# Relu parts of a step put two steps ahead instead of one, in a kernel of 32 dependent steps on four engines

## What is computed

```python
idx = _knn_indices(xyz, K)                        # K = 8, xyz = ctx_4096 (4, 1601, 512)
for i in range(NUM_BLOCKS):                       # 4 blocks, run twice: 8 layers
    shortcut = points                             # (4, 256, 512)
    p = _lrelu(points)                            # slope 0.01
    g = _group_point(p, idx_t)
    c = jnp.einsum('oi,bin->bon', w_center[i], p)
    gn = jnp.einsum('oi,bikn->bokn', w_neighbor[i], g)    # same weights as w_center
    points = (c + gn.sum(axis=2)) / (K + 1.0) + shortcut
```

## Time and profile before

| | |
|---|---|
| time of the runs, median (range) | 353.4 us (353.21 to 355.57), 3 runs |
| the profiled execution's own time | 353.02 us |
| its span, first to last instruction | 351.2 us |
| TensorE busy | 336.7 us (96%) |
| VectorE busy | 239.8 us (68%) |
| ScalarE busy | 129.6 us (37%) |
| GpSimd busy | 84.8 us (24%) |
| granted TensorE clock | full in all 40 slices |

### The profile page before, as it was taken

The page is one execution under the profiler, slowest core; times in us unless marked ns, Lnnn a source line. Parts: engine busy times, 40 slices in busy tenths (PEclk is TensorE's granted clock), DMA queues, the critical chain, the costliest instruction groups (busy, mean ns, idle before and its releaser), DMA issues.

```text
span 351.2 us, 4578 instructions
## 1 busy us (share of the span) xinstructions
PE 336.7 (96%) x1816; PEld 268.3 (76%) x1816; DVE 239.8 (68%) x345; ACT 129.6 (37%) x197; POOL 84.8 (24%) x75
## 2 busy tenths in 40 slices
PE   5999999999999989988899899999999999999996
PEld 2667666666666778877788788888889888888984
DVE  0156378468457474999965877779598687779773
ACT  1116113120411224336445726463552626464410
POOL 2002000200200002225304605243251525235200
PEclk9999999999999999999999999999999999999999
DMA  7994433433120000000000000000000000000023
GB/s 254 336 329 188 149 120 121 149 119 121 55 94 0 3 0 3 0 0 2 0 2 0 0 2 0 3 1 0 2 0 3 0 2 0 2 0 0 10 112 119
DMA packets 7444, 20.20 MB, mean 58 GB/s; under 512 B 640, under 2 KB 1920, under 8 KB 6400
## 3 DMA queue, kind: packets, MB, share of 16 engines
q1 hardware_dynamic: 7424, 19.93, 16.7%
HBM read 17.83 MB, written 2.10 MB: 57 GB/s over the span
## 4 chain that ended last, share of the span: by engine, by line
PE 77%; DVE 13%; ACT 4%; issue 4%; DMA 1%; DVEq 1%
PE wide L249 30%; PE wide L334 24%; PE wide L323 7%; PE wide L312 6%; PE wide L314 6%; DVE y_rest L549 4%; DVE y_lo L553 3%; DVE r_mixed L473 3%; DVE state L561 2%; ACT y_hi L440 2%; PE wide L256 1%; ACT relu L432 1%; DMA points<-in_ctx_dram 1%; PE wide L300 1%; DVE gram L536 1%
## 5 line engine op out<-in xcount | busy, mean ns | idle before, releaser
L232 POOL TENSOR_TENSOR r_low<-relu,r_high 128x512 fp32r<-128x512 f32 x64 | 82.6, 1305 | 245.2 <-ACT r_high L435 245.2
L249 PE MATMUL wide<-points 128*128 128x512 f32 (+3 forms) x384 | 109.9, 440 | 4.1 <-DMA points<-in_ctx_dram 4.1
L334 PE MATMUL wide<-adj,y_hi 128*128 128x512 f32 (+1 forms) x260 | 101.6, 392 | 0.8 <-DVE state L561 0.8
L334 PE MATMUL wide<-adj,y_lo 128*128 128x512 f32 (+1 forms) x260 | 101.4, 391 | 0.0
L249 PEld LDWEIGHTS wide<-points 128*128 128x128 f32 x384 | 65.7, 192 | 38.5 <-issue 19.4
L549 DVE TENSOR_TENSOR y_rest<-wide,y_hi 128x1024 f32<-128x1024 f32 x32 | 39.1, 1221 | 43.5 <-ACT y_hi L440 43.5
L312 PE MATMUL wide<-w_high,r_high 128*128 128x256 f32 x256 | 62.9, 284 | 2.1 <-DVE y_rest L549 1.0
L314 PE MATMUL wide<-w_low,r_low 128*128 128x256 f32 x256 | 62.4, 281 | 0.0
L440 ACT CAST y_hi<-wide 128x1024 fp32r<-128x1024 f32 x32 | 32.2, 1008 | 68.5 <-PE wide L314 68.5
L334 PEld LDWEIGHTS wide<-adj,y_hi 128*128 128x128 f32 x260 | 48.9, 188 | 11.2 <-DVE state L561 1.2
L334 PEld LDWEIGHTS wide<-adj,y_lo 128*128 128x128 f32 x260 | 48.9, 188 | 9.9
(11 more groups left out here) (50 smaller groups left out, 141.9 us busy)
## 6 DMA issues: line engine op xcount, KB each, us to landing
points<-in_ctx_dram SPq DMA_DIRECT2D x8, 1024.0 KB, 5.2
points<-in_ctx_dram SPq DMA_DIRECT2D x8, 256.0 KB, 3.3
points<-in_ctx_dram SPq DMA_DIRECT2D x4, 512.0 KB, 5.5
state<-in_x_dram SPq DMA_DIRECT2D x4, 512.0 KB, 13.3
out_dram<-state SPq DMA_DIRECT2D x3, 512.0 KB, 2.8
rest<-in_ctx_dram SPq DMA_DIRECT2D x8, 128.0 KB, 5.2
w_raw<-in_fside_BxSxS_dram SPq DMA_DIRECT2D x1, 1024.0 KB, 12.6
last_row<-in_ctx_dram SPq DMA_DIRECT2D x1, 1024.0 KB, 16.9
```

Source lines behind the costliest of these rows:

```text
L232: nc.gpsimd.tensor_tensor(r_low[:, b, h, :], relu[:, h, :], r_high[:, b, h, :].bitcast(fp32), ALU.subtract).then_inc(r_low_ready, 1)
L249: mm = nc.tensor.matmul(bank[i][:, 0:N - i * P], points[:, t, i * P:(i + 1) * P], points[:, t, i * P:N], start=(t == 0), stop=False)
L334: mm = nc.tensor.matmul(bank[to][:, cols], part[:, s % 2, q, h * P:(h + 1) * P], adj[:, b, q, cols], start=(q == 0 and part is y_hi), stop ...
```

## The change

A new function `relus_at(s)` says which steps' relu parts stand in step s. Step n gets them two steps ahead (in step n - 2), unless its batch was last updated so late that they can only stand one step ahead: with the previous layer in step p, the place is step max(p + 2, n - 2). ScalarE's `relu_parts` and VectorE's `relu_mixed` both follow it. Their place inside a step is as before (ahead of `y_high(s)`; between the two updates), and TensorE's and GpSimd's instruction order is the same.

```diff
+        def relus_at(s):
+
+            return [n for n in range(B - 1, B * LAYERS)
+                    if s == max(n - 2 if STEPS[n][0] == 0 else step_before(n) + 2, n - 2)]
+
...
             for s in range(B * LAYERS):
-                if s + 1 >= B - 1 and s + 1 <= LAST_STEP:
-                    relu_parts(s + 1)
+                for n in relus_at(s):
+                    relu_parts(n)
                 y_high(s)
...
                     update(s - 1, 0, ALL, 2 * out_at(s - 1), 0)
-                if B - 1 <= s + 1 <= LAST_STEP:
-                    relu_mixed(s + 1)
+                for n in relus_at(s):
+                    relu_mixed(n)
                 if s > 0:
                     update(s - 1, 1, ALL, 2 * out_at(s - 1) + 1, 1)
```

## The result

| | before | with the change |
|---|---|---|
| median of the runs | 353.3 us (353.18 to 355.57, 4 runs) | 372.2 us (371.92 to 372.61, 4 runs) |
| span of the profiled execution | 351.2 us | 370.8 us |
| y_hi of step 0 starts (profiled) | 125.92 | 126.65 |
| from there to the end of the span | 225.3 us | 244.15 us |

The ratio is 1.052, with a 95% interval of 1.048 to 1.056: the change makes the kernel 5% slower. The forecast was 371 us, within 365 to 377. The part ahead of the loop isn't touched by the change, but its length differs from run to run with the first loads (y_hi of step 0 starts between 125.85 and 128.55 us in the profiles of this study), so I compare loops by the stretch from there to the end: 18.9 us more.

The account below looks back on a forecast made before the run. TensorE bounds before, the ring through all engines after. 2.5 us late at the start, 15.0 over six cycles and the end put main(30) 17.7 later: span 368.9, execution 370.7, median 371 us, range 365 to 377.

Parts of the forecast that it names:

- What bounds the kernel: Before the change, TensorE: 6.59 us a step alone, 19.77 for three, where the kernel takes 20.00.
- A to B: From y_hi of the step with two steps' relu parts (A) to the next step's (B): 8.31 us.
- the ring: Turn through all engines, y_hi, y_rest, y_lo, update, r_mixed, update, relu, back to y_hi: 7.17 us before the change.
- B to A': From y_hi of the one-part step (B), through the step with none (C), to the next two-part step (A'): 14.2 us.
- 2.5 us for every three steps: Steady cycle of three steps grows from 20.00 to 22.5 us; six whole cycles add 15.0 us.
- Start: Steps 5 to 9: a late y_hi(5) puts y_hi(9) at 195.3 instead of 192.79, 2.5 us late.
- End: y_hi(27) at 330.3, then 8.31 and 7.17 us to y_hi(29); main(30) at 348.2, 17.7 us later.
- The order of r_mixed and r_low: In the two-part step, VectorE's second r_mixed starts 0.35 us ahead of GpSimd's r_low; no time was added for it.
- the 380 us case: Rival, 7%: GpSimd's r_low gets the port before r_mixed, 1.3 us in each of seven cycles; about 380 us.
- The hold does not go round: Rival, 8%: y_hi of the two-part step is late, the next step's is not; 1.2 us in seven cycles, 362 us.
- Faster: Rival, 3%: r_mixed a step earlier gives back TensorE's 5.1 us of waits, or 3 to 4 of them; 350 us.
- The clock rival: Rival, 1%: TensorE's clock might fall from more waiting, giving far over 380 us.

Follow-up runs that it names:

- the run with two buffers: The change, with two relu buffers instead of one: 368.5 us, ratio 1.043 to the kernel before.
- only the steps four back: Against the kernel before, only steps whose batch was last updated four steps back get their parts a step earlier, on both engines: 354.5 us, ratio 1.003.
- the second r_mixed behind the update: The change, with the second r_mixed of a step behind the second update instead of ahead of it: 368.4 us, ratio 1.041 to the kernel before.
- steps five back alone: Against the kernel before, only steps whose batch was last updated five steps back get their parts a step earlier, on both engines: 370.1 us, ratio 1.048.
- ScalarE's part alone: ScalarE's relu parts as in the change, VectorE's r_mixed as in the kernel before: 370.6 us, ratio 1.049.
- VectorE's part alone: VectorE's r_mixed as in the change, ScalarE's relu parts as in the kernel before: 356.9 us, ratio 1.011.

## Why the prediction was right, point by point

- **What bounds the kernel.** Held. TensorE alone takes 6.59 us a step, and the three kernels that keep ScalarE's old order and only move r_mixed ran at 19.76 us for three.
- **A to B, 8.31 us.** Measured 8.28 in the change and 7.15 where one r_mixed was taken out of the link, as the ring's sum has it. What the link is worth is another matter: with nothing ahead of y_hi(B) A to C takes 12.25 us, with the change 12.87, so it adds 0.6 us. The prediction's times for main(C) say the same, 10.1 by TensorE and 10.7 by y_rest(B); measured were 10.15 and 10.68.
- **B to A', 14.2 us.** Measured 14.23 (4.59 + 9.64), but two of its terms were off and cancelled out, so the agreement within 0.03 us is partly luck. The relu of half 1 can't start at 9.81, because ScalarE is in half 0 until 10.25 (9.04 + 1.21): I left out the engine's own queue there. And I had GpSimd hold back the last relu only; the rows show it at the first relu of the second step too, and smaller in all: 0.29 us of wait in the row at 262.15, and 0.47 us a cycle by the run with two buffers, where the prediction had 13.0 - 12.2 = 0.8.
- **2.5 us for every three steps.** Measured 2.51. The sign given for it, about 2.7 us of idle time of TensorE in three steps, came out at 2.00: the prediction took the whole cycle over 19.77 for idle time, and the profile has TensorE busy for 20.51 of 22.51 us.
- **Start.** y_hi(9) was forecast at 195.3 and came at 197.06. 0.73 us of it is the earlier part of the program, which took that much longer in this run. Two terms were missing. The neighbours' last instruction met GpSimd's r_low in step 5 and took 1.79 us instead of 1.33: from the second update at 171.92 to y_rest(6) at 175.78 it took 3.86 us and not 3.40. And there was a wait that I said I couldn't find: out of step 6 goes into the same PSUM tensor as out of step 5 and must wait for update(5), which came late. TensorE's row:

```profile
180.71 0.50 PE L339 MATMUL wide<-adj,y_hi 128*128 128x512 f32 x1 [0.47 <-DVE state L566]
```

- **End.** y_hi(27) to y_hi(29) 8.29 + 7.14, forecast 8.31 + 7.17.
- **The order of r_mixed and r_low.** r_mixed came first by 0.35 us, as worked out, in every cycle; its mean over the program fell from 1.48 to 1.22 us, and GpSimd paid instead (2.03 for 1.28 us), where nothing waited. So the 380 us case didn't come. The rule of the Trainium skill, SBUF — State Buffer, section "Who interferes with whom", that issue order decides who blocks, agrees with these rows. It agrees too where GpSimd comes first: r_mixed takes 1.80 us in the kernel before and in the one with only the steps four back, and in the one with the second r_mixed behind the update, where that r_mixed starts at 248.02, 0.24 us after an r_low, it takes 2.13 us.
- **The rivals.** "The hold does not go round" asked for a late y_hi(A) and a y_hi(B) on time. The run with steps five back alone is that kernel, and it took 370.1 us, not 362: the rival had one place of the two at which a late y_hi costs TensorE time. "Faster" had y_hi late by less than its slack, which wasn't so. Its gain exists in part: the early r_mixed give back 0.24 us a cycle once ScalarE's part is left alone, 1.8 us in the loop, and not the 3 to 4 us it counted, since most of the 5.1 us lie ahead of the steady part. The clock rival had a mechanism that occurs here, and the wrong size: the clock stayed at 1.00 through the whole steady part, but in two of the change's four runs the mean clock was 0.995, and those two took 372.06 and 371.92 us, no more than the others (372.61 and 372.34). Where it falls, the next section shows.

In the runs with ScalarE's relu parts of two steps in A, other than the change (9.64) and the one with two relu buffers, C to A' is 9.46 or 9.94 us. It is 9.94 where an r_mixed stands between the updates of step C too (ScalarE's part alone, and the steps five back), and the relu of half 1 there waits for the second update, 0.44 us; it is 9.46 where none does (the second r_mixed behind the update).

What stays open: whether the first-part differences of up to 2.7 us come from the chip or from the edits isn't shown (the kernel before has such runs too, 352.0 to 356.0 us). Nor is it shown what decides whether the clock falls after a wait of about 2 us.

## What to carry to other kernels

In an in-order queue an instruction moved earlier is paid by what it is moved past, and "its data is ready" isn't enough: what counts is whether the instruction now behind it has slack for it and for every wait ahead of it. Add up the ring (here y_hi, y_rest, y_lo, update, relu, y_hi) for each distance at which work comes back, compare it with the bounding engine's time for as many steps, and look for a second engine that hangs on the same late instruction. Move the work on the engine that waits idly (VectorE's r_mixed here) and leave it where it is on the one that carries the ring.

## What the runs showed of the hardware

TensorE's granted clock is less safe than I took it to be from the earlier trace rows. It fell after the idle time of 4.32 us in the kernel with VectorE's part alone. It also fell in step 6 of two kernels whose main(6) had waited 1.95 us (ScalarE's part alone, and the second r_mixed behind the update). Main(6) in the one with the second r_mixed behind the update, and its window:

```profile
169.85 0.46 PE L317 MATMUL wide<-w_high,r_high 128*128 128x256 f32 x1 [1.95 <-DVE y_rest L554]
170.11 0.41 PE L319 MATMUL wide<-w_low,r_low 128*128 128x256 f32 x1
170.32 0.41 PE L317 MATMUL wide<-w_high,r_high 128*128 128x256 f32 x1
```

```profile
169.85:177.50 7.65, 7.65 (x38) 7.07 (x39) 7.54 (x10) 3.43 (x5) 3.08 (x2) 0.78 0.00 0
```

The same stretch in the profiled execution of the change, with a wait of 1.93 us ahead of the same matmul:

```profile
167.95 0.36 PE L317 MATMUL wide<-w_high,r_high 128*128 128x256 f32 x1 [1.93 <-DVE y_rest L554]
```

```profile
167.95:175.60 7.65, 6.31 (x37) 5.37 (x38) 7.54 (x9) 3.43 (x5) 3.30 (x2) 1.00 0.00 0
```

At the lower level the matmuls stand 0.21 us apart instead of 0.12, and TensorE is busy for all of the 7.65 us instead of 6.31. So an idle time of nearly the same length lowered the clock in one run and not in another, and in the kernel with the steps five back alone main(10) waited 2.00 us at a clock of 1.00. What it costs depends on the slack: next to nothing with ScalarE's part alone (y_hi(6) to y_hi(7) 8.05 us, the change 8.04), 0.9 us in the kernel shown, and in the kernel with VectorE's part alone seven matmuls that took 0.43 us each instead of 0.23, 1.4 us, besides the idle time itself. In the steady part, with waits of 0.4 to 1.5 us, it never fell in any profile.
